# Two 64-row halves in place of one 128-row contraction in the score matmuls of a cross-attention kernel

## The reference

```python
qh = _split_heads(q @ wq.T + bq, h)
kh = _split_heads(k @ wk.T + bk, h)
vh = _split_heads(v @ wv.T + bv, h)
scores = jnp.einsum('ntd,nsd->nts', qh, kh) / jnp.sqrt(jnp.asarray(depth, qh.dtype))
km = jnp.repeat(mask.astype(scores.dtype), h, axis=0)[:, None, :]
scores = scores + km * PAD
attn = jax.nn.softmax(scores, axis=-1)
ctx = jnp.einsum('nts,nsd->ntd', attn, vh)
out = _merge_heads(ctx, h) + q
mu = jnp.mean(out, axis=-1, keepdims=True)
var = jnp.var(out, axis=-1, keepdims=True)
out = (out - mu) / jnp.sqrt(var + LN_EPS) * gamma + beta
```

## Time and profile before

| | |
|---|---|
| median of 3 runs | 1152.48 us (1152.32 to 1153.96) |
| the profiled execution, its own time | 1157.28 us |
| its span, first to last instruction | 1155.5 us |
| PE busy | 1123.1 us (97%), 7541 matmul records |
| weight loads (PEld) busy | 1037.8 us (90%), 7541 records |
| DVE busy | 822.1 us (71%) |
| POOL busy | 771.8 us (67%) |
| ACT busy | 612.5 us (53%) |

### The profile page before, as it was taken

How to read it: one execution, slowest core, us unless ns; L and a number is a source line. 1 busy time by engine, 2 the same in 40 slices (tenths; PEclk the granted TensorE clock), 3 DMA queues, 4 the chain that set the end, 5 groups by cost and what they waited for, 6 DMA issues and landing times.

```text
span 1155.5 us, 25702 instructions
## 1 busy us (share of the span) xinstructions
PE 1123.1 (97%) x7541; PEld 1037.8 (90%) x7541; DVE 822.1 (71%) x1622; ACT 612.5 (53%) x1008; POOL 771.8 (67%) x667
## 2 busy tenths in 40 slices
PE   7899999999999999999999999999999999999994
PEld 7788789999999999999999999999999999999983
DVE  5776467777777777777777777777777777777786
ACT  3321254556566555555555656655555555565551
POOL 4999523677766676766667776667676666777465
PEclk9999999999999999999999999999999999999996
DMA  7745433233343444343344333344443334333223
GB/s 228 261 147 188 150 104 90 74 122 95 116 119 117 126 126 126 116 120 99 102 123 122 106 105 119 117 126 126 126 116 122 98 102 123 123 101 110 85 82 128
DMA packets 147207, 141.07 MB, mean 122 GB/s; under 512 B 86452, under 2 KB 88004, under 8 KB 147172
## 3 DMA queue, kind: packets, MB, share of 16 engines
q1 hardware_dynamic: 146564, 140.29, 40.1%
q10 hardware_dynamic: 608, 0.33, 0.1%
HBM read 91.71 MB, written 48.85 MB: 122 GB/s over the span
## 4 chain that ended last, share of the span: by engine, by line
PE 84%; DVE 2%; POOL 1%; issue 0%; ACT 0%; DMA 0%; DVEq 0%; SPq 0%; POOLq 0%
PE q_ps L724 31%; PE o_ps L765 23%; PE s_ps L740 18%; PE t_ps L751 12%; POOL x_lo L991 0%; DVE stats L822 0%; DVE attn L853 0%; PE q_ps L765 0%; DVE y L862 0%; DMA xT_raw<-in_xT 0%; DVE attn L814 0%; DVE row_max L885 0%; DVE y L868 0%; ACT q_hi L1030 0%; DVE y L843 0%
## 5 line engine op out<-in xcount | busy, mean ns | idle before, releaser
L765 PE MATMUL o_ps<-v_tiles,pt 128*128 128x66 f32 x2520 | 310.7, 270 | 1.5 <-DVE attn L814 1.5
L765 PEld LDWEIGHTS o_ps<-v_tiles,pt 128*128 128x128 f32 x2520 | 304.0, 192 | 1.9 <-issue 1.9
L885 DVE TENSOR_REDUCE row_max<-s_ps 128x8 f32<-128x616 f32 x256 | 203.2, 794 | 118.2 <-PE s_ps L740 118.1
L740 PE MATMUL s_ps<-bd,q_hi 128*128 128x308 f32 x1024 | 260.5, 305 | 1.1 <-ACT q_hi L1030 1.1
L991 POOL TENSOR_TENSOR x_lo<-xT_raw,x_hi 128x512 fp32r<-128x512 f32 x124 | 159.3, 1286 | 117.8 <-ACT x_hi L1026 117.7
L961 POOL TENSOR_TENSOR attn<-attn,x_rows 128x512 f32<-128x512 f32 x124 | 160.2, 1292 | 115.8 <-DVE attn L814 115.8
L1036 ACT COPY pt<-t_ps 128x512 f32<-128x512 f32 (+1 forms) x320 | 175.0, 588 | 107.1 <-PE t_ps L751 107.0
L1030 ACT ACTIVATE q_hi<-q_ps,bq_col 128x512 fp32r<-128x512 f32 x125 | 86.1, 689 | 254.9 <-PE q_ps L724 254.9
L724 PE MATMUL q_ps<-x_lo,wq_hi 128*128 128x512 f32 x500 | 218.7, 437 | 2.5 <-PEq L142 2.1
L1016 ACT ACTIVATE probs<-probs 128x616 f32<-128x616 f32 x256 | 183.3, 716 | 64.3 <-DVE probs L894 64.3
L894 DVE TENSOR_TENSOR probs<-s_ps,row_max 128x616 f32<-128x616 f32 x256 | 204.6, 799 | 5.7
(11 more groups left out here) (96 smaller groups left out, 1292.9 us busy)
## 6 DMA issues: line engine op xcount, KB each, us to landing
xT_raw<-in_xT SPq DMA_DIRECT2D x128, 256.0 KB, 3.5
x_rows<-in_x SPq DMA_DIRECT2D x32, 1024.0 KB, 5.6
out<-y SPq DMA_DIRECT2D x128, 256.0 KB, 2.1
k_scratch<-k_out SPq DMA_DIRECT2D x8, 1232.0 KB, 5.4
bd<-k_scratch SPq DMA_DIRECT2D x128, 77.0 KB, 2.4
v_scratch<-v_out SPq DMA_DIRECT2D x16, 264.0 KB
v_tiles<-v_scratch SPq DMA_DIRECT2D x256, 9.9 KB
ctx_raw<-in_ctxT SPq DMA_DIRECT2D x3, 1232.0 KB, 6.2
```

The costliest lines, as they stand in the source:

```text
L740: mm = pe.matmul(s_ps[t % 2][:, j, 0:GS], (q_hi, q_lo)[u][:, g, P * t:P * t + P], bd[par][:, v, g, :, :].rearrange("p h s -> p (h s)"), st ...
L765: mm = pe.matmul(bank_of(b, t)[:, col:col + tile_cols[i]], pt[h][0:w, i, P * t:P * t + P], v_tiles[v_buffer(b, h)][0:w, i, 0:tile_cols[i]] ...
L885: dve.tensor_reduce(row_max[:, u, :].rearrange("p (j h) -> p j h", j=2), score_heads(t), AX.X, ALU.max).then_inc(max_ready, 1)
```

## The change

Each score matmul of 128 rows and 308 columns becomes two, r = 0 and 1, each of the 64 rows of one half of the partitions and of 2 x 77 = 154 columns (`PS = 2 * S`): the two heads that these rows hold. The half r writes bank r of s_ps, the group j the columns from 154 j of it. The two halves use different rows of the array and different banks. bd has two head slots in place of four, and head q goes to slot q % 2 of its rows, so bd is half as large. To leave the heads in the order in which everything behind the scores expects them, the host permutes wq, wk, their biases and a second copy of the mask (`mask_k`, read by `load_mask`) by `by_slot`. The layout of s_ps that DVE reads stays: two banks with 308 columns each.

```diff
-        bd0 = sb(whole, "bd0", [P, 2, NG, HG, S], F32R)
+        bd0 = sb(whole, "bd0", [P, 2, NG, 2, S], F32R)
...
-            bd = [bd0, sb(two, "bd1", [P, 2, NG, HG, S], F32R)]
+            bd = [bd0, sb(two, "bd1", [P, 2, NG, 2, S], F32R)]
...
-                        sp.dma_start(bd[par][rows, :, :, q, :].bitcast(F32), k_dram[b, rows, :, :, :]
+                        sp.dma_start(bd[par][rows, :, :, q % 2, :].bitcast(F32), k_dram[b, rows, :, :, :]
...
                         for n, (u, v) in enumerate(terms):
-                            mm = pe.matmul(s_ps[t % 2][:, j, 0:GS], (q_hi, q_lo)[u][:, g, P * t:P * t + P],
-                                           bd[par][:, v, g, :, :].rearrange("p h s -> p (h s)"),
-                                           start=(n == 0), stop=(n == 2))
+                            for r in range(2):
+                                rows = slice(P // 2 * r, P // 2 * r + P // 2)
+                                mm = pe.matmul(s_ps[t % 2][:, r, PS * j:PS * j + PS],
+                                               (q_hi, q_lo)[u][rows, g, P * t:P * t + P],
+                                               bd[par][rows, v, g, :, :].rearrange("p h s -> p (h s)"),
+                                               start=(n == 0), stop=(n == 2))
                     mm.then_inc(scores_done, 1)
...
+    def by_slot(a, width):
+        a = np.asarray(a)
+        return a.reshape(2, 2, 2, 2, width, -1).transpose(0, 2, 1, 3, 4, 5).reshape(a.shape)
...
+        "mask_k": c(by_slot(np.asarray(mask_BxS2_ik0).reshape(HEADS, 2, S), 1)),
-        "wqT": c(np.asarray(L0_xattn_wq).T),
+        "wqT": c(by_slot(L0_xattn_wq, D // HEADS).T),
```

More of the change, by code:

```diff
@@ L25, in at_least, with xattn @@
     eng.wait_ge(sem, value)
-def xattn(nc, x, xT, ctxT, mask, wqT, bq, wkT, bk, wvT, bv, gamma, beta, out):
+def xattn(nc, x, xT, ctxT, mask, mask_k, wqT, bq, wkT, bk, wvT, bv, gamma, beta, out):
     B, T, D = x.shape
@@ L41, in xattn @@
     GS = HG * S
+    PS = 2 * S
     CB = 8
@@ L210, in load_keys @@
                         rows = slice(DH * q, DH * q + DH)
-                        sp.dma_start(bd0[rows, :, :, q, :].bitcast(F32), k_dram[b, rows, :, :, :]).then_inc(k_loaded[0], DMA)
+                        sp.dma_start(bd0[rows, :, :, q % 2, :].bitcast(F32), k_dram[b, rows, :, :, :]).then_inc(k_loaded[0], DMA)
                 def store_values(c, first, end):
@@ L336, in load_mask @@
                 def load_mask():
-                    mask_heads = mask.rearrange("(g q) i s -> q g (i s)", q=HG)
+                    mask_heads = mask_k.rearrange("(g q) i s -> q g (i s)", q=HG)
                     for q in range(HG):
@@ L1089 @@
         "mask": c(np.asarray(mask_BxS2_ik0).reshape(HEADS, 2, S)),
-        "wqT": c(np.asarray(L0_xattn_wq).T),
-        "bq": c(np.asarray(L0_xattn_bq).reshape(D // 128, 128).T),
-        "wkT": c(np.asarray(L0_xattn_wk).T),
-        "bk": c(np.asarray(L0_xattn_bk).reshape(D // 128, 128).T),
+        "mask_k": c(by_slot(np.asarray(mask_BxS2_ik0).reshape(HEADS, 2, S), 1)),
+        "wqT": c(by_slot(L0_xattn_wq, D // HEADS).T),
+        "bq": c(by_slot(L0_xattn_bq, D // HEADS).reshape(D // 128, 128).T),
+        "wkT": c(by_slot(L0_xattn_wk, D // HEADS).T),
+        "bk": c(by_slot(L0_xattn_bk, D // HEADS).reshape(D // 128, 128).T),
         "wvT": c(np.asarray(L0_xattn_wv).T),
```

## The result

The changed kernel takes 1186.73 us (median of 4 runs, 1185.28 to 1190.97), the kernel before 1153.22 us. The ratio is 1.0291, with a 95% interval from 1.0255 to 1.0326: 33.5 us slower. The forecast was 1196 us and slower. The profiled execution took 1186.03 us, with a span of 1184.0 us. The spans of the two profiled executions differ by less, 28.5 us: that of the kernel before had the lower mean granted clock, 0.988 against 0.994, which makes up some 7 us (an estimate, 0.012 x 1155.5 less 0.006 x 1184.0). From step to step in the loop (eight groups of scores, mean from 200 to 1000 us) the traces have 31.29 us before and 32.37 us now, which over 32 batch elements is 34 us.

The account below looks back on a forecast made before the run. PE, busy 97% of the span, was taken as the bound. Per group 0.20 + 0.59 + 0.07 + 0.16 = 1.02 us against 0.845, +0.175 us, times 256 +44.8, less 1.1, gave 1196 us; range 1140 to 1385 us.

Parts of the forecast that it names:

- The side-by-side loads: In the scores, the weight loads of a pair's two halves run beside each other; with holds at the edges, 40%.
- B: Rival: loads of the halves follow one another, with holds at the edges; +0.815 us a group, 1360 us; chance 30%.
- the upper edge: Upper of two values for a pair of side-by-side loads, 0.112 and 0.124 us; the middle, 0.118 us, was taken.
- five pairs: In each score group, the five pairs of half matmuls after the first, 5 x 0.118 = 0.59 us.
- C: Rival: loads of the halves in turn, but no hold at the edges; +0.465 us a group, 1270 us; chance 10%.
- The hold at the edges: At each change of array shape, two a group, the next load is held until 0.09 us behind the stream.
- the way in: From q matmuls into the half-array scores: 0.09 us held plus 0.11 us of load laid open, 0.20 us a group.
- The way out: From scores to transposes or product: 0.09 us held plus the open load (0.06 or 0.11), together 0.16 us a group.
- the MEMSET: POOL's MEMSET of bd, 2.16 us, halves and shortens PE's wait for q_hi: 1.1 us off, once.
- Rival D: Faster: loads side by side and no hold at the edges; -0.175 us a group, 1106 us; chance 15%.
- point of decision: For a faster kernel with 0.118 us a pair, the two edges together must cost less than 0.18 us.
- Nothing else late: Outside the scores: DVE, ACT and POOL get more idle time, and no wait is added to any engine.

Follow-up runs that it names:

- Wide216: The changed kernel with each half matmul streaming 216 columns in place of 154: 1192.53 us, ratio 1.0321.
- r_all: The changed kernel with all six matmuls of the lower half ahead of all six of the upper one: 1261.72 us, ratio 1.0931.
- dummies: The kernel before with one 16-column matmul ahead of each sub-step's scores: 64 rows 1253.75 us, 128 rows (control) 1182.26 us, 32 rows 1254.66 us.
- r_outer: The changed kernel with the loops over halves and terms swapped, three matmuls of the lower half, then three of the upper: 1191.69 us, ratio 1.0326.
- pair: The odd token tile's scores moved on PE directly behind the even one's: in the changed kernel 1176.00 us, in the kernel before 1178.62 us.
- ssqq: Both tiles' scores, then both halves of the q projection, put first on PE: in the changed kernel 1182.73 us, in the kernel before 1196.25 us.
- sq_full: The kernel before with both tiles' scores together, transposes and a product between the two q halves: 1166.17 us; the changed kernel in this order 1150.71 us.

## Why the prediction was right

**The side-by-side loads** were the open question, and the odds I gave (40% against 30% for B) fell the right way; nothing in the rows had settled it. Pairs stand 0.11 us apart, the upper edge being 0.124. I took 0.118 and 0.111 was right: five pairs, 0.035 us a group, 9 us too much. Wide216 shows that this is the load. Rivals B (1360 us) and C are out: their time needs loads one after another, which only r_all made, in part.

**The hold at the edges**, taken from a single place with 16 rows, came true at 0.09 us behind the stream on the way in. I priced the way in at 0.20 us. By the rows above, pair two runs at 507.17 and pairs are 0.11 us apart, so pair one really ran from 507.06, 0.16 us behind the end of the q stream at 506.90: I had counted the load's full 0.11 us where only 0.07 stood open. The way out was forecast at 0.16 us. In the chain, what follows the scores grew by 0.14 and 0.15 us (transposes, three sub-steps of four) and by 0.20 us (the product, the fourth), 0.16 us on the mean, but that agreement is of the chain's making. Its pieces go from recorded end to recorded end, and a half matmul's record ends 0.20 us behind its stream (507.89 and 507.69), a q matmul's 0.17 us (507.07 and 506.90): 0.03 us of the way out lie in the 0.82 us of the scores. The way out cost 0.19 us, since the load was held 0.13 us there and not 0.09. Sum by the streams: in 0.16, five pairs 0.56, the last stream 0.07, out 0.19, together 0.98 us; by the chain 0.82 + 0.16, the same. I had 1.02, so it is +0.135 us a group and 35 us in all; the forecast had +0.175 and 44.8. Less the MEMSET, which came as foretold (1.13 us), 34 us against the measured 33.5. That it fits so well owes something to luck: I had 0.04 us too much for the way in, 0.03 too much for the pairs and 0.03 too little for the way out.

The dummies confirm the edges without any half scores, 0.28 us for both over a control.

**Rival D**, the faster one, failed at the hold alone. Its point of decision was edges under 0.18 us, and they cost 0.16 + 0.19 = 0.35 us. With the whole group at 0.135 us over the 0.845 us of before, the edges are still too dear, though pairs were cheaper than I had them.

**Nothing else late**: DVE, ACT and POOL have the same busy time in a longer span, and PE gained no wait. (What I called all nine waits of PE are nine rows with eleven waits; nothing hangs on it.) The size was off by 10 us of 33.5, on the three terms named.

**What I had wrong afterwards**: that pairs are made by neighbours in the program (r_outer), and that an order is free if the sums of times between producer and consumer fit (pair, ssqq). In pair and ssqq a result was needed exactly where the moved work had stood as cover, and sq_full shows a remainder of it in one pair of four.

## What to carry to other kernels

In this kernel, splitting a contraction into row tiles halved the streams, not the loads. With 128 stationary columns of float32r a load was 0.11 us, so a half matmul of 154 columns (0.07 us) was bound by its load, and a pair of them replaced one full matmul of 0.14 us by 0.11: a gain of 0.03 us for each pair. Each run of row-tiled matmuls between full ones then paid about 0.3 us for going in and out (0.28 by the dummies; 0.135 + 6 x 0.03 = 0.31 in the changed kernel), so a run must be long (here 24 half matmuls just paid, 12 did not), and before work is moved to make it long, look for what that work was hiding.

## What the runs showed that I had not expected

The two halves of the array took their matmuls like two queues: with three of one half ahead of three of the other in the program, both still started in one record's time (r_outer, 1191.69 us), and only with six ahead did the second half come late, by 0.29 us (r_all, 1261.72 us). The price of a change of shape was the same for a 32-row and a 64-row part (1254.66 and 1253.75 us).
